# A two-layer graph attention network on one core: both units' scores issued together, a transposed linear part, half the combining products, and another wait for the gathers

## The reference

```
h   = layer_norm(x)
xl  = (h @ Wl + bl) as 2 heads x 128;  xr = (h @ Wr + br) as 2 heads x 128
e   = leaky_relu(xl[src] + xr[dst], 0.2)             # one row for each edge and head
score = sum over d of e * att
alpha = softmax of score over the edges of one dst
g   = sum over the edges of one dst of alpha * xl[src]  + gat_b
x   = x + g @ proj_W + proj_b
x   = x + gelu(layer_norm(x) @ W1 + b1) @ W2 + b2
```

## Time and profile before

| | |
|---|---|
| time, median of 3 runs | 2720.81 us (2719.72 to 2721.34) |
| the profiled execution's own time | 2717.65 us |
| its span (first to last instruction) | 2716.0 us |
| PE / PEld busy | 2270.8 us (84%) / 1455.6 us (54%) |
| DVE / ACT busy | 1314.9 us (48%) / 1427.9 us (53%) |
| POOL busy | 1546.4 us (57%) |
| mean granted TensorE clock | 0.970 of full speed |

### The profile page before, as it was taken

How to read it: one execution, slowest core, us unless ns; L and a number is a source line. 1 busy time by engine, 2 the same in 40 slices (tenths; PEclk the granted TensorE clock), 3 DMA queues, 4 the chain that set the end, 5 groups by cost and what they waited for, 6 DMA issues and landing times. The chain is left out here.

```text
span 2716.0 us, 70339 instructions
## 1 busy us (share of the span) xinstructions
PE 2270.8 (84%) x20985; PEld 1455.6 (54%) x20985; DVE 1314.9 (48%) x5318; ACT 1427.9 (53%) x3474; POOL 1546.4 (57%) x1664
## 2 busy tenths in 40 slices
PE   4588888988988988988847888888888888888885
PEld 2345555555555555655534555555555555555554
DVE  7334454545545545554543344444444444444544
ACT  4334555555555555555533455555555555555554
POOL 4666666566566566665326666666665666666650
PEclk9799999999999999999978999999999999999996
DMA  5544444444444444444224444444444444444430
GB/s 136 166 124 127 125 134 129 131 134 128 130 134 129 131 133 131 130 131 131 67 65 127 127 124 125 128 125 126 128 124 127 127 124 128 126 125 128 125 105 8
DMA packets 236764, 332.92 MB, mean 123 GB/s; under 512 B 51010, under 2 KB 160490, under 8 KB 236394
## 3 DMA queue, kind: packets, MB, share of 16 engines
q0 software_dynamic: 75072, 208.30, 29.1%
q1 hardware_dynamic: 161322, 120.16, 15.3%
HBM read 308.02 MB, written 20.25 MB: 121 GB/s over the span
## 5 line engine op out<-in xcount | busy, mean ns | idle before, releaser
L980 POOL DMA_INDIRECT rows<-table,src_t x1564 | 1495.4, 956 | 975.1 <-issue 335.9
L1200 ACT ACTIVATE lz<-psum 128x512 f32<-128x512 f32 x782 | 469.9, 601 | 993.9 <-PE psum L1087 524.7
L1429 DVE SCALAR_TENSOR_TENSOR acc<-acc,keep,psum 128x129 f32 x782 | 273.3, 349 | 900.7 <-remote 764.1
L1102 PE MATMUL psum<-ident,rows 128*128 128x128 f32 x3128 | 533.8, 288 | 115.9 <-issue 81.2
L1087 PE MATMUL psum<-lz,att_w 128*32 128x256 f32 x3128 | 531.4, 396 | 87.7 <-issue 67.7
L1102 PEld LDWEIGHTS psum<-ident,rows 128*128 128x128 f32 x3128 | 344.6, 143 | 407.3 <-issue 369.9
L1176 PE MATMUL psum<-rows,wgt 128*32 128x129 f32 x6256 | 274.0, 281 | 83.4 <-DVE acc L1429 68.0
L1105 PE MATMUL psum<-oh,xrw 96*128 96x256 bf16 x1564 | 304.4, 276 | 4.9 <-issue 4.9
L1080 PE MATMUL psum<-ident,lin 128*128 128x128 f32 x1568 | 282.3, 303 | 7.6 <-issue 7.2
L1280 ACT ACTIVATE ex<-hold_s,peak 128x256 f32<-128x256 f32 x392 | 201.4, 514 | 165.1 <-issue 146.6
L1327 DVE TENSOR_SCALAR oh<-relb,win_col,less 128x256 bf16<-128x256 int16 x782 | 232.3, 366 | 73.4 <-DMA table<-row 29.7
(11 more groups left out here) (257 smaller groups left out, 2193.2 us busy)
## 6 DMA issues: line engine op xcount, KB each, us to landing
xrw<-xr_split SPq DMA_DIRECT2D x782, 48.0 KB
relb<-rel_d SPq DMA_DIRECT2D x194, 192.0 KB
rows<-table,src_t POOLq DMA_INDIRECT x1564
relb<-cyc_d SPq DMA_DIRECT2D x194, 64.0 KB
xr_split<-split SPq DMA_DIRECT2D x50, 192.0 KB, 1.9
table<-row SPq DMA_DIRECT2D x50, 130.0 KB, 2.0
x_mid<-x SPq DMA_DIRECT2D x25, 64.0 KB
xo<-x_mid SPq DMA_DIRECT2D x25, 64.0 KB
```

The source lines that it names most:

```text
L980: pool.indirect_dma_start(rows[:, ring(u), t, u % M, :, :].rearrange("p h c -> p (h c)"), None, s["tables"][layer][0:NP, :], bass.Indirect ...
L1102: pe.matmul(z[:, o:o + P], rows[:, ring(u), t, u % M, h, 0:D], s["ident"][:, :], is_transpose=True, start=(h == 0 and t == 0), stop=False, ...
L1200: act.activation(lz[:, u % M, :], ps[u % M][:, :], ACT.Relu).then_inc(lz_ready, 1)
L1429: m = v.scalar_tensor_tensor(a, a, s["keep"][:, u:u + 1], sum_bank(i - 8)[:, c:c + D + 1], ALU.mult, ALU.add)
```

## The change

TensorE's order in an iteration becomes: sums; the whole score of step i-1 for both units; project even; project odd; node work; transposes of `ex`. In the score the linear part is issued in transpose mode, and the four products with `att_w` of the two units stand one behind the other, behind one wait for both units' relu. The selection matrices hold both heads side by side, so that a combining product writes 64 rows instead of 32; half as many are issued, and the two iterations now do half of the nodes each, instead of a head each. ScalarE's copy to `gT` reads the other layout. On GpSimd, the gathers of an odd unit of step g wait from step 9 on for `sums_ready` of g-8, which TensorE raises in iteration g-2, instead of for `z_ready` of iteration g-3.

```diff
@@ gpsimd
             for u in range(NU):
-                if u >= 3 * M:
+                if u >= 3 * M and (u % M == 0 or step_of(u) <= 8):
                     pool.wait_ge(z_ready, u - 3 * M + 1)
+                elif u >= 3 * M:
+                    pool.wait_ge(sums_ready, step_of(u) - 8)
@@ tensor: score
-            def score(u):
-                g = u // M
-                at = u % M * HW
+            def score(g):
                 out = scores(g)
-                if u % M == 0:
-                    n = len(of_step(g)) * HW
-                    hold(pe, held, g - 1)
-                    pe.wait_ge(lin_ready, g + 1)
-                    for t in range(K):
-                        pe.matmul(out[0:n, t * P:t * P + P], lin[:, g % 2, t, 0:n], s["ident"][:, :],
-                                  start=(t == 0), stop=False, skip_group_check=True)
-                pe.matmul(out[at:at + HW, 0:UE], s["mask_w"][:, :], oh[:, u % (3 * M), :],
-                          start=False, stop=False, skip_group_check=True)
-                pe.wait_ge(lz_ready, u + 1)
-                for h in range(H):
-                    o = at + h * W
-                    m = pe.matmul(out[o:o + W, 0:UE], w["att_w"][:, h * W:h * W + W],
-                                  lz[:, u % M, h * UE:h * UE + UE], start=False, stop=True, skip_group_check=True)
-                if u == of_step(g)[-1]:
-                    m.then_inc(score_ready, 1)
+                n = len(of_step(g)) * HW
+                hold(pe, held, g - 1)
+                pe.wait_ge(lin_ready, g + 1)
+                for t in range(K):
+                    pe.matmul(out[0:n, t * P:t * P + P], lin[:, g % 2, t, 0:n], s["ident"][:, :], is_transpose=True,
+                              start=(t == 0), stop=False, skip_group_check=True)
+                for u in of_step(g):
+                    at = u % M * HW
+                    pe.matmul(out[at:at + HW, 0:UE], s["mask_w"][:, :], oh[:, u % (3 * M), :],
+                              start=False, stop=False, skip_group_check=True)
+                pe.wait_ge(lz_ready, min(g * M + M, NU))
+                for u in of_step(g):
+                    for h in range(H):
+                        o = u % M * HW + h * W
+                        m = pe.matmul(out[o:o + W, 0:UE], w["att_w"][:, h * W:h * W + W],
+                                      lz[:, u % M, h * UE:h * UE + UE], start=False, stop=True, skip_group_check=True)
+                m.then_inc(score_ready, 1)
@@ tensor: combining
-                        for m in range(P // W):
+                        for m in range(2):
                             for c in range(3):
-                                mm = pe.matmul(bank(t)[m * W:m * W + W, h * (D + 1):h * (D + 1) + D + 1],
-                                               s["sel"][:, h, c, :], stg[t % 2][:, 2 * m + c, :], start=(c == 0),
+                                mm = pe.matmul(bank(t)[m * HW:m * HW + HW, q * (D + 1):q * (D + 1) + D + 1],
+                                               s["sel"][:, c, :, :].rearrange("p h w -> p (h w)"),
+                                               stg[t % 2][:, 2 * (2 * q + m) + c, :], start=(c == 0),
                                                stop=(c == 2), skip_group_check=True)
@@ tensor: iteration i, behind the sums
-                for j in range(M):
-                    if (i - 1) * M + j in of_step(i - 1):
-                        score((i - 1) * M + j)
-                    if j == M - 1:
-                        node_work(i)
-                    if i * M + j in of_step(i):
-                        project(i * M + j)
-                    if j == 0 and of_step(i - 5):
+                if of_step(i - 1):
+                    score(i - 1)
+                for u in of_step(i):
+                    project(u)
+                node_work(i)
+                if of_step(i - 5):
```

More of the change, by code:

```diff
@@ L84, in gnn @@
         mask_w = sb("mask_w", [P, HW], BF16)
-        sel = sb("sel", [P, H, 3, W], F32)
+        sel = sb("sel", [P, 3, H, W], F32)
         fresh = sb("fresh", [P, NU + 1], F32)
@@ L1132, in node_work @@
                                   ).then_inc(next_proj, 1)
-                for h, tl in [(0, nodes(i, -1)), (1, nodes(i, 0))]:
+                for q, tl in [(0, nodes(i, -1)), (1, nodes(i, 0))]:
                     for t in tl:
@@ L1178, in _ @@
                     m.then_inc(sums_ready, 1)
-                for j in range(M):
-                    if (i - 1) * M + j in of_step(i - 1):
-                        score((i - 1) * M + j)
-                    if j == M - 1:
-                        node_work(i)
-                    if i * M + j in of_step(i):
-                        project(i * M + j)
-                    if j == 0 and of_step(i - 5):
-                        pe.wait_ge(ex_ready, i - 4)
-                        hold(pe, wgt_ready, i - 5)
-                        for t in range(K):
-                            m = pe.transpose(ps[4][:, t * P:t * P + P], ex[:, (i - 5) % 2, t * P:t * P + P],
-                                             s["ident"][:, :])
-                        m.then_inc(ex_turned, 1)
+                if of_step(i - 1):
[4 more added lines that the diff above has]
+                if of_step(i - 5):
+                    pe.wait_ge(ex_ready, i - 4)
+                    hold(pe, wgt_ready, i - 5)
+                    for t in range(K):
+                        m = pe.transpose(ps[4][:, t * P:t * P + P], ex[:, (i - 5) % 2, t * P:t * P + P],
+                                         s["ident"][:, :])
+                    m.then_inc(ex_turned, 1)
         @block.scalar
```

13 lines of the change are left out of this document (7 added, 6 removed).

## The result

Where the forecast was made the change makes the kernel slower: 2743.67 us median of 4 runs (2740.19 to 2745.98) beside 2721.07 (2719.72 to 2722.51) for the kernel before, ratio 1.008 (95% interval 1.0068 to 1.0091). The forecast was 2632. Later groups of runs came from chips of two kinds. On the first kind the kernel before takes 2719 to 2722 us, as here. On the second it takes 2299 us, and there the change makes it faster: 2216.24 us beside 2299.49, ratio 0.9643 (0.9629 to 0.9657). That ratio leaves out two of the 15 executions of the kernel before, of 2603 and 2867 us, in which the granted clock was 0.74 and 0.65 instead of 0.97. After this result the first kind was met on three chips and the second on two, each chip once. So "kind" is a name for what was seen there; whether it stays with the chip isn't shown.

A forecast was written before the change was run, and what follows sets the result against it. GpSimd's rows of four gathers plus the delay before TensorE's results are seen were taken as the bound. Saving 76 us in the steps and 12 at the ends, 88 in all, gave 2632 us; own range 2600 to 2665, wider 2490 to 2775.

The forecast's parts named there:

- What bounds the kernel: Steps inside both layers: GpSimd's four gathers plus late visibility of TensorE's results set the step, 4.71 + 1.54 = 6.25 us.
- TensorE's own step: TensorE's work per step falls from 4.5 to 3.6 us; the combining group halves; hidden by GpSimd inside the stretches.
- The row begun by the sums, 6.10 us: Ordinary steps: rows of four stay, and GpSimd starts with VectorE's accumulation, saving 0.15 us: 6.25 to 6.10 us.
- Covered by the 2.5 us left in the step: End of iteration: moving `ex` transposes last delays the joined score to 1.6 us after a release, claimed to cost nothing.
- The split steps, 76 us with the shorter row: Steps split into pairs at combined tiles vanish; all 338 go from mean 6.325 to 6.10 us, saving 76 us.
- The ends, 12 us: Behind each layer's last gather, TensorE's saved work is uncovered: 6 us a layer, 12 us in all (bounds 0 and 20).
- Pairs everywhere: Rival: z not visible when the odd pair ends, so GpSimd stops twice a step; 6.50 us a step, 2765 us; chance 0.24.
- Short waits, or none: Rival: splitting lets TensorE's results out earlier; 2590 us with short waits, 2257 with none; chance 0.22 for under 2600.
- TensorE at the lower clock: Rival: less TensorE activity lowers its clock in the layers; 2770 us; chance 0.05, shared with rows that come too late.

The follow-up runs named there:

- experiment 8: Kernel before with only TensorE's new order and the joined score; old products, combining and waits; first kind: 2918.45 us, ratio 1.0726.
- experiment 4: Changed kernel with both units' relus ahead of ScalarE's copy to `wgt`; first kind: 2722.04 us, ratio 1.0009 against the kernel before.
- experiment 1: Changed kernel with both units' gathers waiting for `z_ready` as before the change; first kind: 2720.36 us, ratio 1.0002 against the kernel before.
- experiment 2: Kernel before with only the odd unit's gathers waiting for `sums_ready` from step 9 on; first kind: 2779.84 us, ratio 1.023.
- experiment 3: Kernel before with only the transposed linear part and halved combining; first kind, three chips: 2712.58, 2709.67 and 2714.32 us.
- experiment 5: Changed kernel with old `z_ready` waits and both relus ahead of the copy: ratio 1.0021 on first kind, 0.9635 on second, against the kernel before.

## Why the prediction was wrong

*What bounds the kernel* (right on the first kind, not on the second). That GpSimd's row and the lateness behind it set the step was confirmed on the first kind by halving the gathers (6.33 to 5.33 us) and by 115 us less TensorE in a stretch that holds the same 652 gathers. I had taken the lateness for a property of the kernel. It is one of the kernel where it runs: on the second kind the same program has none. By what means it arises, and what differs between the chips, no run shows.

*TensorE's own step* (right). 0.9 us less was forecast, and the halved combining beside it. With halved gathers TensorE's busy time falls from 5.32 to 4.19 us a step, by 1.12 with the combining included. The eight products of the score take 0.64 us (805.05), as forecast, and the combining group has 12 instructions.

*The row begun by the sums, 6.10 us* (a term of the sum that failed). VectorE's accumulation and GpSimd's start did come together (805.16 and 805.28, 0.12 us apart, as said), but the row was no shorter. The step at 805.28 to 811.45 takes 6.17, the 174 rows of four 6.27 on average, against 6.28 before. The 0.15 us that I took off GpSimd's start came back as a later accumulation: behind a row's end it started at 1.37 us (median) instead of 1.27. The other 159 of 334 steps broke into pairs.

*"Covered by the 2.5 us left in the step"* (the step of the mechanism that failed). I listed this chain myself: `ex`, copy to `wgt`, odd relu, joined score. I counted it from the release, 1.6 us, and set it against the gathers' row. But the pair's end, 2.5 us behind the release, is the time by which z has to be seen, and this chain puts score and both projections at or behind the release, 805.05 to 807.16, where before the even unit's products needed no odd relu. Where the score began behind the release, 155 of 183 rows broke; where it began ahead of it, 4 of 151. The even z of the broken rows ended at 2.60 us (median). In 74 of those 159 rows it ended in time and was seen too late. Where `ex` falls behind the release as well, a whole row is lost (experiment 8).

Experiment 4 takes the copy out of the chain and gets 19 of the 22 us back with all else unchanged; experiment 1 gets 21 back by making the row insensitive to it. Either one suffices, so the changed kernel's loss needs both: a late z, and a trigger that splits the row for it. On the kernel before, with its longer TensorE work, each of the two costs by itself and more (61 us in experiment 2, 199 in experiment 8), so the parts don't add up to the whole.

*The split steps, 76 us with the shorter row* (mis-sized: the stretches became 22 us longer). I took the pairs for the cost. In the kernel before a step in pairs costs only 0.2 us more than a row of four (6.48 against 6.28), and a row of four that has to wait for late TensorE work can cost more. Experiment 1 has no pairs, and its step is 6.34 us, not 6.10 and not below before's 6.33. Experiment 2 has few and costs 61 us.

*The ends, 12 us* (mis-sized: 2 us). Between the last gather of layer 0 and the first of layer 1 there are 82.1 us after (1336.75 to 1418.87) and 85.4 before (1322.85 to 1408.23), 3.3 us less. Behind the last gather of layer 1 it is 1.4 us more: it starts at 2661.00 after, and its end is 78.7 us ahead of the end of the span; before, from 2637.72 + 0.95, it is 77.3 us. TensorE has fewer products there, but some of them run slower than the 0.64 us of 805.05:

```profile
2663.97 1.06 PE L1089 MATMUL psum<-lz,att_w 128*32 128x256 f32 x8 [1.99 <-ACT lz L1200]
...
2665.87 0.63 PE L1106 MATMUL psum<-oh,xrw 96*128 96x256 bf16 x2
```

*The rivals.* "Pairs everywhere" named the right mechanism, late z behind the odd relu, and its point, release to z of 2.9 us against 2.5. It happened in part: 318 rows of two are 159 steps in pairs, where before had 171 / 2, some 85. A step in pairs takes 6.55 us, near the 6.50 that I gave it. The 74 more of them by 0.28 us over a row of four are 21 us, and the 85 that there were before by 0.07 more are 6; rows of four that are 0.01 shorter take 2 off. That is 25 us, near the 22 lost in the stretches. "Short waits, or none" at 2257 us is near what the second kind shows (2216), by another cause than I gave. "TensorE at the lower clock": the clock did fall, to 0.86. It costs little by itself, as experiments 1 and 4 run at 0.91 and 0.88 in the layers and take as long as the kernel before at 1.00. But it makes a late z later (2.55 us from score to z instead of 1.45), and of the late scores below the full clock 89 of 93 broke their row, of those at it 66 of 90. How much of the 22 us would be left at the full clock, no run shows.

*The clock.* In experiment 3 TensorE was busy 903 of 1032 us beside 913 in the earlier trace rows, and its clock fell from 1.00 to 0.96:

```profile
208.00:1240.00 1032.00, 903.10 (x7863) 534.39 (x7863) 519.75 (x2142) 571.70 (x1396) 630.26 (x654) 0.96 0.47 131
```

In experiment 2, with 890 us busy and the old products, it was 0.98. The Trainium skill (TensorE: Matmul & The Clock Gate, Part 4) says that transposes don't count as activity for the full clock; the two rows agree in direction, but no run changed the transposes alone.

## What to carry to other kernels

Where the results of one engine are seen late for a stretch, ask of each result on which side of that stretch it falls: a chain that is moved by 1 us can cost a whole row (experiment 8), and work that is saved elsewhere gives next to nothing (experiments 1 and 3). Don't put a copy that waits for a late result ahead of a short operation that others need, above all where the trigger depends on that operation: experiment 4 gained 19 us by it, experiment 5 on the first kind nothing. Let a trigger stand on one kind of event, the earliest that is safe. And profile the kernel before again when its time on a chip differs: the same change was 0.8% slower on one chip and 3.6% faster on another, and the two traces of before show what bounds it on each.

## What the runs showed of the hardware that I had not expected

The kernel before takes 2719 to 2722 us on some chips and 2299 us on others, with the same program. On the first kind most of TensorE's completions that fall late into a row of four gathers 1.25 us apart come out 0.9 to 1.4 us after the row's end (VectorE's accumulation in the kernel before: median 1.27 us of 253), some earlier, as the copy at 804.13, 0.31 us after it. On the second they are seen within 0.05 us in an unbroken sequence of gathers.

The wait behind a row grows with the row. Over ten traces of the first kind with all gathers, layers' starts included, GpSimd pauses 0.98 us behind rows of two (median of 1271), 1.55 behind four (3113), 1.72 behind six (35), 2.3 behind eight (8) and 3.14 behind sixteen (3.02 to 3.30, 20 of them). In the kernel before on the second kind it pauses 0.6 us behind rows of 22 and of 30.

TensorE itself stands still there. In the kernel before, ahead of 274 of the 422 releases in the two stretches, it paused, mostly for 0.3 to 1.2 us, with nothing that the profile shows it waiting for. It went on 1.04 us behind the row's end and 0.50 us ahead of GpSimd (medians); the same kernel on the second kind has no such pause ahead of its releases. One is in the step of the earlier trace rows:

```profile
807.75 0.60 PE L1102 MATMUL psum<-ident,rows 128*128 128x128 f32 x4 [1.06 <-issue]
```

So it isn't settled whether only the news of TensorE's results is late on the first kind, or TensorE is held up too.

The delay does not hold each result in the changed kernel: after 805.28 the z of 806.12 + 0.38 = 806.50 was read at 806.74, inside the row,

```profile
806.12 0.38 PE L1106 MATMUL psum<-oh,xrw 96*128 96x256 bf16 x2
...
806.74 0.61 ACT L1200 ACTIVATE lz<-psum 128x512 f32<-128x512 f32 x1
```

while the transposes that ended at 807.82 were read at 811.05. From which gather on, or which result, the lateness begins was not settled. With half the gathers, nearly always one at a time (732 of 748 rows in the kernel before on the first kind), it did not show: 5.33 us a step on both kinds, and 4.53 and 4.54 with the change.
